# A two-layer relational graph convolution: separate PSUM banks for the halves of the turn, one bank for node sums, one DRAM table of sums for both layers

## The chip, the cores and the metric

The kernel runs on one core of one Trainium2 chip. The metric is the device time of one execution in microseconds (us). A line number such as L1712 is a line of the kernel file before the change. Engines: PE is TensorE, DVE is VectorE, ACT is ScalarE, POOL is GpSimd, SP is SyncE.

## The reference

There are 50000 nodes with 128 features, 50000 edges sorted by destination, each with 128 attributes and one of 8 types.

```python
h = relu(layernorm(x))
for l in range(2):
    m = relu(h[src] + edge_attr)                         # one row for each edge
    seg = edge_type * N + dst
    mean = segment_sum(m, seg) / max(count(seg), 1)      # a mean for each node and type
    h = einsum('rnd,rdo->no', mean.reshape(8, N, 128), weight[l]) + h @ root[l] + bias[l]
    h = batch_norm(h)                                    # over all nodes
    if l == 0: h = relu(h)
out = x + h
```

## The kernel before, in words

**Tiles and groups.** The edges are cut into 394 tiles of 127 (plus one of overlap); four tiles, far apart in the list, make one of NG = 99 groups. `tiles(g)` names the tiles of group g. Each layer l runs one loop over the groups, with all engines some groups apart; `gg = l * NG + g` counts on through both layers. A step of the loop is called step i here.

**What happens to a group.** POOL gathers the source rows of its four tiles with one indirect DMA each (L839) into a ring `hb`. In layer 0 DVE and ACT normalise them (L1145 to L1165, L1465); in layer 1 DVE scales and shifts them (L1179, L1180). DVE adds the edge rows, loaded by SP (L699), and signals `t_ready` (L1176, L1182). DVE also makes one matrix for each tile, `pm`, which orders the edges by type into 8 x 32 slots and scales them by one over the count (L1193, function `columns`, signal `set_ready`). Then comes **the turn** (function `turn`, L1702 to L1718): for each tile one product of 128x128 by 128x256 that turns the rows so that features lie on partitions and edges lie ordered by type. A group has two halves of two tiles, h = 0 and h = 1; each half fills one PSUM bank of 128x512. ACT takes a half out with Relu (function `message`, L1485, signal `m_ready`, two for each group). The end of half 0 is signalled as `half_ps`, of half 1 as `tr_ps`. **In the kernel before both halves go to the one bank `ps_turn` = `ps_t[0]`**, so each half waits for the message of the half before it (L1709: `m_ready` >= 2*gg + h).

After the turn PE multiplies by the weights of each type (`products`, L1745, banks `ps_y[0]` and `ps_y[1]`, signals `yh_ps` and `y_ps`), ACT copies each bank out (`products_out`, L1493), PE turns it back (`turned_back`, L1777, banks `ps_s`), ACT copies the first half (`first_half`, L1502) and DVE the second (`second_half`, L1257), and PE sums over edges of the same node with a 0/1 matrix `sm` that DVE made (`same_node`, L1219): `node_sums`, L1791, into `ps_o[gg % 2]`. ACT copies row 0 of these sums into the input of the next group (`carry`, L1515, signal `carried`) and the whole bank to a buffer `ob` (`sums_out`, L1524, signal `ob_ready`). POOL scatters `ob` to the table `acc[l]` with one indirect DMA for each tile (L854); for the tiles named WIDE, SP writes 112 rows with a plain DMA (L723). In layer 0, PE also makes one column of places for each tile and half (`place_column`, L1731, bank `ps_t[1]`, signal `place_ps`); in layer 1 it multiplies early rows by the root matrix (`first_rows` L1802, `first_product` L1807, bank `ps_t[1]`).

**Order by hand.** Each engine runs its instructions in the order in which they are written. PE's step i (L1810 to L1831) is: products(i, 0) with the place columns of group i+1 between them, turned_back(i-1, 0), turn(i+2, 0), [first_rows], products(i, 1), turned_back(i-1, 1), turn(i+2, 1), [first_product], node_sums(i-2). ACT's step i (L1539 to L1563) is: carry(i-2), sums_out(i-3), root_of(i+4), [first_turned, first_out], products_out(i, 0), first_half(i-1), message(i+2, 0), normalised(i+4), products_out(i, 1), message(i+2, 1), half_normalised(i+4). DVE's step i (L1278 to L1303) is: group_stats(i+4), edge_sum(i+3), columns(i+3), group_scales(i+4), same_node(i-1), places_in(i+1), second_half(i-1); the stats, scales and places are there in layer 0 only. In `columns`, DVE waits for `place_ps` of group i+1 (layer 0) before it overwrites `pm`.

**POOL's order** (L899 to L902): the scatters of group after group, with gathers put between them. Before the scatters of group g it waits for `ob_ready` (L845), and before the third tile's it waits for `tr_ps` >= gg + 6, the end of turn(g+5, 1) (L848).

**The tables of sums.** `acc` has two tables, one for each layer, of 25 MB each that must be zero where nothing is scattered. ACT zeroes `acc[0]` during the setup with 28 DMAs (L1449); SP zeroes `acc[1]` during the loop of layer 0, one DMA of 896 KB every third step (L744). After each loop, three rows are added where the streams of tiles meet (L882), and a pass over 49 chunks of nodes reads the table, adds the product with the root matrix and, in layer 0, stores the rows `h1_rows` for the next layer. All engines have a second program for edges that aren't sorted; with this input it isn't taken.

Of the kernel before, what the change touches and what calls it, by code (L numbers as in the profile page):

```python
# [41 lines left out]
def gnn_kernel(nc, x, src, dst, edge_attr, edge_type, weight, root, bias, gamma, beta, out):  # L42
# [105 lines left out]
    with ctx:  # L148
# [11 lines left out]
        acc = [dram(f"acc_{l}", [P * F + NTP * P, D]) for l in range(L)]  # L160
# [285 lines left out]
        ps_turn = ps_t[0]  # L446
# [219 lines left out]
        def _(sp):  # L666
# [36 lines left out]
            edge_rows(0, 0)  # L703
            edge_rows(1, 0)
# [109 lines left out]
        def _(pool):  # L814
# [74 lines left out]
            def layers(put):  # L889
# [17 lines left out]
            with pool.If(unsorted > 0):  # L907
# [10 lines left out]
                layers(scatter_alone)  # L918
# [14 lines left out]
        def _(dve):  # L933
# [186 lines left out]
            def in_order(sorted_):  # L1120
# [5 lines left out]
                def counts_in():  # L1126
                    dve.wait_ge(inv_ps, 5)
                    own.link(v.tensor_copy(inv_t[:, :], ps_t[1][:, :]))
                    own.link(v.memset(inv_t[0:1, :], 1.0))
# [73 lines left out]
                def places_in(g):  # L1203
                    w = len(tiles(g))
                    dve.wait_ge(place_ps, g + 1)
                    at = ps_t[1][:, 0:NH * H].rearrange("p (b j) -> p b j", b=NH)
# [64 lines left out]
                def join_rows():  # L1271
                    dve.wait_ge(join_to_ps, 1)
                    v.tensor_copy(join_at[:, :], ps_t[1][0:J, W4 - 1:W4]).then_inc(join_at_ready, 1)
# [159 lines left out]
        def _(act):  # L1433
# [43 lines left out]
            def message(g, h, l):  # L1477
# [7 lines left out]
                a_.activation(mt_at(gg)[:, a:b, :].rearrange("p j c -> p (j c)"), ps_turn[:, 0:(b - a) * RC],  # L1485
# [19 lines left out]
            def carry(g, l):  # L1505
# [7 lines left out]
                else:  # L1513
                    act.wait_ge(o_ps, sums_done(l, g - 1))
                    a_.activation(to, ps_o[(gg - 1) % 2][0:1, 0:w * D], ACT.Copy).then_inc(carried, 1)  # L1515

            def sums_out(g, l):
# [6 lines left out]
                a_.activation(ob[:, gg % OB, 0:w, :].rearrange("p w d -> p (w d)"), ps_o[gg % 2][:, 0:w * D],  # L1524
                              ACT.Copy).then_inc(ob_ready, 1)

            def first_turned(k):
# [3 lines left out]
                a_.activation(ht[:, k % 2, 0:W4], ps_t[1][:, :], ACT.Relu, scale=bn_col[:, 0, 0:1],  # L1531
                              bias=bn_col[:, 0, 1:2]).then_inc(ownT_ready, 1)

            def first_out(k):
                act.wait_ge(first_ps, k + 1)
                a_.activation(own_at(k // 2)[:, k % 2 * W4:(k % 2 + 1) * W4], ps_t[1][:, :], ACT.Copy).then_inc(first_ready, 1)
# [100 lines left out]
        def _(pe):  # L1637
# [57 lines left out]
            def program(sorted_):  # L1695
# [4 lines left out]
                cols(ps_t[1], tm_inv).then_inc(inv_ps, 1)  # L1700

                def turn(g, h, l):  # L1702
# [6 lines left out]
                    wait(pe, m_ready, 2 * gg + h)  # L1709
                    for j in range(a, b):  # L1710
                        if sorted_:
                            last = te.matmul(ps_turn[:, (j - a) * RC:(j - a + 1) * RC], hb[:, hb_slot(gg), j, :], pm[:, gg % 2, j, :],  # L1712
                                             start=True, stop=True)
                        else:
                            for c in range(NH):
                                k = (j - a) * RC + c * P
                                last = te.transpose(ps_turn[:, k:k + P], hb[:, hb_slot(gg), j, :], ident[:, :])
                    last.then_inc((half_ps, tr_ps)[h], 1)  # L1718

                def place_column(g, n):  # L1720
# [10 lines left out]
                    last = te.matmul(ps_t[1][:, k:k + 1], pm[:, g % 2, j, b * P:(b + 1) * P], ikey_t[:, t:t + 1], start=True, stop=True)  # L1731
# [50 lines left out]
                def node_sums(g, l):  # L1782
# [12 lines left out]
                def first_rows(k):  # L1795
# [4 lines left out]
                    for j in range(H):  # L1800
                        a = (k % 2 * H + j) * D
                        last = te.transpose(ps_t[1][:, j * D:(j + 1) * D], own_at(i)[:, a:a + D], ident[:, :])  # L1802
                    last.then_inc(ownT_ps, 1)

                def first_product(k):
                    pe.wait_ge(ownT_ready, k + 1)
                    te.matmul(ps_t[1][:, :], root_sb[:, D:2 * D], ht[:, k % 2, 0:W4], start=True, stop=True).then_inc(first_ps, 1)  # L1807
# [156 lines left out]
```

## Time and profile before

| what | us |
|---|---|
| median of 3 timed runs | 2876.24 |
| lowest and highest of them | 2862.11, 2884.39 |
| the profiled execution, its own time | 2859.57 |
| its span (first to last instruction) | 2857.8 |
| outside the span | 1.8 |

The profile is of one execution. Busy shares are of the span. In a row of the waits, "PE ps_t L1712 <- ACT arena L1485" means that PE stood idle before line 1712 until ACT's line 1485 released it. "remote" stands where the signal came at a time at which no recorded instruction ended, and "issue" where the engine waited for nothing that the profile shows.

### The profile page before, as it was taken

The numbers are of one execution on the slowest core, as the hardware profiler recorded it, in microseconds if no ns is written. First come the engines' busy times: TensorE is split into PE (matmuls) and PEld (weight loads), VectorE is DVE, ScalarE is ACT, GpSimd is POOL, SyncE is SP. The second block draws the span as 40 slices with busy tenths as digits, with TensorE's granted clock in tenths as the row PEclk, the third lists the DMA queues.
The fourth block names the chain that finished last, engine by engine and source line by source line (L and its number), as shares of the span: only waits on it lengthen the run. The fifth ranks groups of instructions, "written<-read, shape, count | busy, mean of one in ns | idle before, by whom it ended". The sixth has DMA issues, their size and how long they took to land. (4 is left out here: it accounts for less than half of the span.)

```text
span 2857.8 us, 43800 instructions
## 1 busy us (share of the span) xinstructions
PE 2128.6 (74%) x14404; PEld 1932.0 (68%) x14404; DVE 1557.2 (54%) x4526; ACT 1296.7 (45%) x2670; POOL 1406.9 (49%) x1377
## 2 busy tenths in 40 slices
PE   2168878777777777778996777887778787787966
PEld 0058777677677777767995666776667676677955
DVE  4565556555555555553786555554454454444754
ACT  0035556555555555554442344444343344343555
POOL 6405444555455555554003576676676677762100
PEclk9998999998988989988997898998898788998976
DMA  9423444444344433432996233322222233217889
GB/s 340 157 96 109 122 133 135 133 125 132 126 133 132 132 124 104 128 114 95 408 415 226 69 101 93 90 84 85 85 82 84 75 90 90 83 52 266 287 337 404
DMA packets 264672, 434.29 MB, mean 152 GB/s; under 512 B 39075, under 2 KB 170782, under 8 KB 264444
## 3 DMA queue, kind: packets, MB, share of 16 engines
q1 hardware_dynamic: 196598, 251.61, 26.0%
q0 software_dynamic: 46192, 99.84, 12.2%
q10 hardware_dynamic: 21654, 79.99, 6.9%
q8 instruction: 121, 1.98, 0.3%
q14 instruction: 107, 0.88, 0.1%
HBM read 255.41 MB, written 175.88 MB: 151 GB/s over the span
## 5 line engine op out<-in xcount | busy, mean ns | idle before, releaser
L854 POOL DMA_INDIRECT acc<-arena x550 | 585.6, 1065 | 732.8 <-PE ps_t L1712 454.8
L1712 PE MATMUL ps_t<-arena 128*128 128x256 f32 x1576 | 492.3, 441 | 414.0 <-ACT arena L1485 318.6
L1712 PEld LDWEIGHTS ps_t<-arena 128*128 128x128 f32 x1576 | 302.8, 214 | 490.4 <-ACT arena L1485 331.4
L839 POOL DMA_INDIRECT arena<-h_rows,arena x394 | 416.6, 1057 | 327.5 <-DMA h_rows<-chunk_mem 182.2
L1193 DVE TENSOR_SCALAR arena<-arena 128x256 f32<-128x256 f32 x788 | 274.6, 412 | 486.7 <-remote 414.6
L1745 PE MATMUL ps_y<-arena 128*128 128x128 f32 (+1 forms) x3168 | 518.1, 292 | 16.5 <-issue 16.1
L1791 PEld LDWEIGHTS ps_o<-arena 128*128 128x128 f32 x3152 | 476.1, 231 | 49.1 <-issue 33.4
L1493 ACT ACTIVATE arena<-ps_y 128x512 f32<-128x512 f32 (+1 forms) x396 | 231.4, 584 | 546.2 <-remote 489.1
L1791 PE MATMUL ps_o<-arena 128*128 128x128 f32 x3152 | 471.0, 313 | 7.5 <-issue 7.5
L1745 PEld LDWEIGHTS ps_y<-arena 128*128 128x128 f32 x3168 | 445.5, 201 | 27.9 <-issue 18.5
L839 POOL DMA_INDIRECT arena<-in_x_dram,arena x394 | 387.0, 982 | 135.8 <-issue 121.4
L1257 DVE COPY arena<-ps_s 128x512 f32<-128x512 f32 (+1 forms) x198 | 136.3, 689 | 361.9 <-remote 288.3
L1219 DVE TENSOR_TENSOR arena<-arena 128x512 f32<-128x512 f32 (+1 forms) x396 | 254.4, 684 | 110.9 <-remote 68.9
L1485 ACT ACTIVATE arena<-ps_t 128x512 f32<-128x512 f32 x396 | 233.4, 589 | 160.6 <-PE ps_t L1712 78.3
L1777 PE MATMUL ps_s<-ident,arena 128*128 128x128 f32 x1576 | 256.1, 281 | 28.8 <-issue 28.1
L1515 ACT ACTIVATE arena<-ps_o 1x512 f32<-1x512 f32 (+1 forms) x196 | 113.6, 580 | 303.1 <-remote 147.1
L1777 PEld LDWEIGHTS ps_s<-ident,arena 128*128 128x128 f32 x1576 | 195.5, 150 | 38.1 <-issue 37.9
L1731 PEld LDWEIGHTS ps_t<-arena 128*128 128x128 f32 x1576 | 214.7, 198 | 2.7 <-issue 2.5
L1731 PE MATMUL ps_t<-arena 128*128 128x1 f32 x1576 | 203.9, 233 | 2.9 <-issue 1.5
L1465 ACT ACTIVATE arena<-arena,nmr,rstd 128x128 f32<-128x128 f32 x394 | 162.1, 484 | 30.3 <-DVE nmr L1165 30.3
L1502 ACT ACTIVATE arena<-ps_s 128x512 f32<-128x512 f32 (+1 forms) x198 | 116.0, 586 | 92.1 <-PE ps_s L1777 46.0
L1524 ACT ACTIVATE arena<-ps_o 128x512 f32<-128x512 f32 (+1 forms) x198 | 112.4, 567 | 7.6 <-remote 5.6
(280 smaller groups left out, 2396.6 us busy)
## 6 DMA issues: line engine op xcount, KB each, us to landing
arena<-in_edge_attr_dram SPq DMA_DIRECT2D x190, 256.0 KB
chunk_mem<-acc SPq DMA_DIRECT2D x55, 512.0 KB, 13.2
acc<-arena ACTq DMA_DIRECT2D x28, 896.0 KB
acc<-arena SPq DMA_DIRECT2D x28, 896.0 KB
arena<-in_x_dram SPq DMA_DIRECT2D x45, 512.0 KB, 9.7
arena<-acc SPq DMA_DIRECT2D x43, 512.0 KB, 10.6
chunk_mem<-hn_rows SPq DMA_DIRECT2D x41, 512.0 KB
out_dram<-arena ACTq DMA_DIRECT2D x38, 512.0 KB, 9.2
```

What stands on the lines that cost most here:

```text
L839: pool.indirect_dma_start(out=hb[:, hb_slot(gg), t // NG, :], out_offset=None, in_=(x, h1_tab)[l], in_offset=at(src_t[:, t:t + 1])).then_i ...
L854: pool.indirect_dma_start(out=acc[l], out_offset=at(idx_t[:, t:t + 1]), in_=ob[:, gg % OB, t // NG, :], in_offset=None, **how).then_inc(co ...
L1193: ins = v.tensor_scalar(pm[:, gg % 2, j, :], iota_f[:, :], slot_t[:, t:t + 1], inv_t[:, t:t + 1], ALU.is_equal, ALU.mult)
L1219: ins = v.tensor_tensor(sm[:, gg % SM, b, 0:w, :], iota_f[:, 0:P].unsqueeze(1).to_broadcast([P, w, P]), place_at[:, g, b, 0:w].unsqueeze(2 ...
L1465: ins = a_.activation(row, row, ACT.Relu, scale=rstd[:, g % 2, j:j + 1], bias=nmr[:, g % 2, j:j + 1])
L1485: a_.activation(mt_at(gg)[:, a:b, :].rearrange("p j c -> p (j c)"), ps_turn[:, 0:(b - a) * RC], ACT.Relu).then_inc(m_ready, 1)
L1493: a_.activation(yts[:, gg % 2, b, 0:w, :].rearrange("p j e -> p (j e)"), ps_y[b][:, 0:w * D], ACT.Copy).then_inc(yt_ready, 1)
L1712: last = te.matmul(ps_turn[:, (j - a) * RC:(j - a + 1) * RC], hb[:, hb_slot(gg), j, :], pm[:, gg % 2, j, :], start=True, stop=True)
L1731: last = te.matmul(ps_t[1][:, k:k + 1], pm[:, g % 2, j, b * P:(b + 1) * P], ikey_t[:, t:t + 1], start=True, stop=True)
L1745: last = te.matmul(to[:, 0:w, q, :], w_sb[l][:, r * D:(r + 1) * D], mt_at(gg)[:, 0:w, r * CAP:(r + 1) * CAP], start=True, stop=True)
L1777: last = te.transpose(ps_s[b][:, c], yts[:, gg % 2, b, j, :], ident[:, :])
L1791: last = te.matmul(ps_o[gg % 2][:, c], sm[:, gg % SM, b, j, :], yb[:, gg % 2, b, j, :], start=b == 0, stop=b == NH - 1)
```

## The change

Six edits. (1) The turn's half h writes bank `ps_t[h]`, and its wait is one message shorter: half 0 waits for message(g-1, 0), half 1 for message(g-1, 1). (2) Node sums have one bank, `ps_o[0]`, so `node_sums` waits until sums_out of the group before it is done (`ob_ready` >= gg in place of gg - 1). (3) What used `ps_t[1]` (places, early rows, counts, joins) uses `ps_o[1]`, named `ps_side`. (4) Both layers scatter to one table `acc`; SP's 28 zeroing DMAs in layer 0 go, and so does POOL's wait for them. Both layers write the same rows of it, so that layer 1 overwrites what layer 0 left. (5) SP issues the edge rows of groups 2 and 3 with those of 0 and 1, ahead of its wait for the counts. (6) In the program for unsorted edges POOL zeroes the table again between the layers.

```diff
-        acc = [dram(f"acc_{l}", [P * F + NTP * P, D]) for l in range(L)]
+        acc = [dram("acc", [P * F + NTP * P, D])] * L
...
-        ps_turn = ps_t[0]
+        ps_sum = ps_o[0]
+        ps_side = ps_o[1]
...
-            edge_rows(0, 0)
-            edge_rows(1, 0)
+            for g in range(XB):
+                edge_rows(g, 0)
...
-                sp.wait_ge(acc_zero[l], 16 * ZN)
+                if l == 0:
+                    sp.wait_ge(acc_zero[0], 16 * ZN)
                 for n in range(NG):
-                    if l > 0 or n >= 2:
+                    if l > 0 or n >= XB:
                         edge_rows(n, l)
...
-                    if l == 0 and n % 3 == 0 and n // 3 < ZN:
-                        far = bass.AP(acc[1].tensor, (n // 3) * P * ZW, [[ZW, P], [1, ZW]])
-                        sp.dma_start(far, zeros[:, :]).then_inc(acc_zero[1], 16)
...
+            def zero_again():
+                for a in range(ZN):
+                    pool.dma_start(bass.AP(acc[1].tensor, a * P * ZW, [[ZW, P], [1, ZW]]), zeros[:, :]).then_inc(acc_zero[1], 16)
+                pool.wait_ge(acc_zero[1], 16 * ZN)
...
                         all_stored(pool)
+                        if again is not None:
+                            again()
...
-                        pool.wait_ge(acc_zero[1], 16 * ZN)
...
-                layers(scatter_alone)
+                layers(scatter_alone, zero_again)
...
                 # message (ACT)
-                a_.activation(mt_at(gg)[:, a:b, :]..., ps_turn[:, 0:(b - a) * RC],
+                a_.activation(mt_at(gg)[:, a:b, :]..., ps_t[h][:, 0:(b - a) * RC],
...
                 # carry and sums_out (ACT)
-                    a_.activation(to, ps_o[(gg - 1) % 2][0:1, 0:w * D], ACT.Copy).then_inc(carried, 1)
+                    a_.activation(to, ps_sum[0:1, 0:w * D], ACT.Copy).then_inc(carried, 1)
...
                 # turn (PE)
-                    wait(pe, m_ready, 2 * gg + h)
+                    wait(pe, m_ready, 2 * gg - 1 + h)
                     for j in range(a, b):
                         if sorted_:
-                            last = te.matmul(ps_turn[:, (j - a) * RC:(j - a + 1) * RC], hb[:, hb_slot(gg), j, :], pm[:, gg % 2, j, :],
+                            last = te.matmul(ps_t[h][:, (j - a) * RC:(j - a + 1) * RC], hb[:, hb_slot(gg), j, :], pm[:, gg % 2, j, :],
...
                 # node_sums (PE)
-                    wait(pe, ob_ready, gg - 1)
+                    wait(pe, ob_ready, gg)
...
-                            last = te.matmul(ps_o[gg % 2][:, c], sm[:, gg % SM, b, j, :], yb[:, gg % 2, b, j, :],
+                            last = te.matmul(ps_sum[:, c], sm[:, gg % SM, b, j, :], yb[:, gg % 2, b, j, :],
```

## Rows read from the trace of the kernel before

**Rows 1.** Page: busy time of each engine, share of the span, instructions.

```profile
PE 2128.6 (74%) x14404; PEld 1932.0 (68%) x14404; DVE 1557.2 (54%) x4526; ACT 1296.7 (45%) x2670; POOL 1406.9 (49%) x1377
```

**Rows 2.** Windows (us, each engine's busy us, granted clock, DMA share, GB/s).

```profile
230.00:1310.00 1080.00, 837.76 (x5775) 787.19 (x5773) 601.77 (x2537) 605.87 (x1407) 558.74 (x557) 0.90 0.41 125
...
1357.00:1510.00 153.00, 148.20 (x1321) 145.85 (x1321) 125.48 (x300) 67.42 (x146) 0.00 (x0) 1.00 1.02 412
...
1550.00:2580.00 1030.00, 783.62 (x4980) 689.19 (x4980) 509.70 (x975) 422.19 (x777) 696.95 (x648) 0.87 0.30 84
```

**Rows 3.** Windows of line 1524 alone, one sums_out for each step.

```profile
230.00:1310.00 1080.00, 51.23 (x90) 0.90 0.41 125
...
1550.00:2580.00 1030.00, 55.24 (x97) 0.87 0.30 84
```

**Rows 4.** Waits in 230 to 1310 us: total us, times, longest.

```profile
DVE arena L1193 <- remote: 387.9, 74, 7.9
POOL acc L854 <- PE ps_t L1712: 367.7, 90, 5.7
ACT arena L1493 <- remote: 309.8, 70, 6.8
...
PE ps_t L1712 <- ACT arena L1485: 220.1, 78, 5.0
```

**Rows 5.** Timeline, one step of layer 0, start, us, engine, line.

```profile
712.39 0.47 PE L1745 MATMUL ps_y<-arena 128*128 128x128 f32 x2
...
714.03 0.99 POOL L854 DMA_INDIRECT acc<-arena  x1 [0.30 <-issue]
...
716.33 0.60 ACT L1493 ACTIVATE arena<-ps_y 128x512 f32<-128x512 f32 x1 [4.45 <-remote]
716.82 0.59 ACT L1502 ACTIVATE arena<-ps_s 128x512 f32<-128x512 f32 x1
717.30 0.60 ACT L1485 ACTIVATE arena<-ps_t 128x512 f32<-128x512 f32 x1
717.96 1.13 PE L1712 MATMUL ps_t<-arena 128*128 128x256 f32 x4 [1.45 <-ACT arena L1485]
718.92 1.95 PE L1791 MATMUL ps_o<-arena 128*128 128x128 f32 x16
719.37 0.98 POOL L854 DMA_INDIRECT acc<-arena  x1 [4.35 <-PE ps_t L1712]
...
722.17 0.57 ACT L1515 ACTIVATE arena<-ps_o 1x512 f32<-1x512 f32 x1
722.64 0.57 ACT L1524 ACTIVATE arena<-ps_o 128x512 f32<-128x512 f32 x1
...
723.24 1.06 POOL L839 DMA_INDIRECT arena<-in_x_dram,arena  x1 [0.30 <-issue]
```

**Rows 6.** Waits in 1550 to 2580 us, the loop of layer 1.

```profile
PE ps_t L1712 <- ACT arena L1485: 91.2, 32, 11.7
...
POOL acc L854 <- PE ps_t L1712: 74.5, 32, 5.4
```

**Rows 7.** Timeline of PE inside a long run of POOL's DMAs, layer 1.

```profile
1934.27 0.37 PE L1777 MATMUL ps_s<-ident,arena 128*128 128x128 f32 x1 [0.63 <-issue]
1934.98 0.46 PE L1777 MATMUL ps_s<-ident,arena 128*128 128x128 f32 x1 [0.34 <-issue]
1935.69 0.37 PE L1777 MATMUL ps_s<-ident,arena 128*128 128x128 f32 x1 [0.25 <-issue]
```

**Rows 8.** Line 744 (zeroing), and the waits of SP's queue.

```profile
L744 SPq DMA_DIRECT2D acc<-arena x28: 18/432/1454, 160.9 to 1058.4; - x28
...
SPq L699 <- DVE arena L1176: 511.0, 61, 11.1
```

More of the change, by code:

```diff
@@ L887, in _, with layers @@
                 gather(g, t, 0)
-            def layers(put):
+            def zero_again():
+                for a in range(ZN):
+                    pool.dma_start(bass.AP(acc[1].tensor, a * P * ZW, [[ZW, P], [1, ZW]]), zeros[:, :]).then_inc(acc_zero[1], 16)
+                pool.wait_ge(acc_zero[1], 16 * ZN)
+            def layers(put, again=None):
                 for l in range(L):
@@ L1127, in counts_in @@
                     dve.wait_ge(inv_ps, 5)
-                    own.link(v.tensor_copy(inv_t[:, :], ps_t[1][:, :]))
+                    own.link(v.tensor_copy(inv_t[:, :], ps_side[:, :]))
                     own.link(v.memset(inv_t[0:1, :], 1.0))
@@ L1272, in join_rows @@
                     dve.wait_ge(join_to_ps, 1)
-                    v.tensor_copy(join_at[:, :], ps_t[1][0:J, W4 - 1:W4]).then_inc(join_at_ready, 1)
+                    v.tensor_copy(join_at[:, :], ps_side[0:J, W4 - 1:W4]).then_inc(join_at_ready, 1)
                 for l in range(L):
@@ L1530, in first_turned @@
                     act.wait_ge(first_ps, k - 1)
-                a_.activation(ht[:, k % 2, 0:W4], ps_t[1][:, :], ACT.Relu, scale=bn_col[:, 0, 0:1],
+                a_.activation(ht[:, k % 2, 0:W4], ps_side[:, :], ACT.Relu, scale=bn_col[:, 0, 0:1],
                               bias=bn_col[:, 0, 1:2]).then_inc(ownT_ready, 1)
@@ L1535, in first_out @@
                 act.wait_ge(first_ps, k + 1)
-                a_.activation(own_at(k // 2)[:, k % 2 * W4:(k % 2 + 1) * W4], ps_t[1][:, :], ACT.Copy).then_inc(first_ready, 1)
+                a_.activation(own_at(k // 2)[:, k % 2 * W4:(k % 2 + 1) * W4], ps_side[:, :], ACT.Copy).then_inc(first_ready, 1)
             for l in range(L):
@@ L1699, in program @@
                 pe.wait_ge(tminv_in, 32)
-                cols(ps_t[1], tm_inv).then_inc(inv_ps, 1)
+                cols(ps_side, tm_inv).then_inc(inv_ps, 1)
                 def turn(g, h, l):
@@ L1716, in turn @@
                                 k = (j - a) * RC + c * P
-                                last = te.transpose(ps_turn[:, k:k + P], hb[:, hb_slot(gg), j, :], ident[:, :])
+                                last = te.transpose(ps_t[h][:, k:k + P], hb[:, hb_slot(gg), j, :], ident[:, :])
                     last.then_inc((half_ps, tr_ps)[h], 1)
@@ L1730, in place_column @@
                     k = b * H + j
-                    last = te.matmul(ps_t[1][:, k:k + 1], pm[:, g % 2, j, b * P:(b + 1) * P], ikey_t[:, t:t + 1], start=True, stop=True)
+                    last = te.matmul(ps_side[:, k:k + 1], pm[:, g % 2, j, b * P:(b + 1) * P], ikey_t[:, t:t + 1], start=True, stop=True)
                     if n == NH * w - 1:
@@ L1801, in first_rows @@
                         a = (k % 2 * H + j) * D
-                        last = te.transpose(ps_t[1][:, j * D:(j + 1) * D], own_at(i)[:, a:a + D], ident[:, :])
+                        last = te.transpose(ps_side[:, j * D:(j + 1) * D], own_at(i)[:, a:a + D], ident[:, :])
                     last.then_inc(ownT_ps, 1)
@@ L1806, in first_product @@
                     pe.wait_ge(ownT_ready, k + 1)
-                    te.matmul(ps_t[1][:, :], root_sb[:, D:2 * D], ht[:, k % 2, 0:W4], start=True, stop=True).then_inc(first_ps, 1)
+                    te.matmul(ps_side[:, :], root_sb[:, D:2 * D], ht[:, k % 2, 0:W4], start=True, stop=True).then_inc(first_ps, 1)
                 for l in range(L):
@@ L1833, in program @@
                             pe.wait_ge(join_set, 1)
-                            te.matmul(ps_t[1][0:J, W4 - 1:W4], join_to[:, :], ones[0:1, 0:1], start=True, stop=True).then_inc(join_to_ps, 1)
+                            te.matmul(ps_side[0:J, W4 - 1:W4], join_to[:, :], ones[0:1, 0:1], start=True, stop=True).then_inc(join_to_ps, 1)
                         if sorted_ and l == 0 and i == -1:
```

6 lines of the change are left out of this document (3 added, 3 removed).

## The prediction, written before the changed kernel was run

> **What bounds the kernel now.** I read the page first: no engine is busy for more than 74% of the span [rows 1], so the time lies in waits. Then the windows by stage. The two loops over groups take 1080 us of layer 0 and 1030 us of layer 1; the pass between them is bound by DMA (share 1.02) and runs at the full clock [rows 2]. Line 1524 runs once for each step, so the windows hold 90 and 97 steps [rows 3]: a step is 1080 / 90 = 12.0 us in layer 0 and 1030 / 97 = 10.6 us in layer 1. Against that stand two floors. PE is busy for 837.76 / 90 = 9.3 us of a step and 783.62 / 97 = 8.1 us. POOL is busy for 558.74 us and has 0.30 us of issue ahead of each of its 557 instructions [rows 2, 5], together 726 us or 8.1 us a step; in layer 1 it is 696.95 + 648 x 0.30 = 891 us or 9.2 us a step. So layer 0 lies 2.7 us over its floor (PE) and layer 1 lies 1.4 us over its own (POOL).
>
> The waits of layer 0 say who waits for whom: POOL waits 367.7 us, 4.1 us a step, for the turn; PE's turn waits 220.1 us (78 times, 2.8 us each) for the message; ACT's products_out waits 309.8 us for something "remote" and DVE's columns 387.9 us [rows 4]. One step shows it as a ring [rows 5]. PE's last product that ACT waits for is listed to end at 712.86, but ACT starts its copy at 716.33. POOL's run of indirect DMAs ended at 715.02. The same order stands in the other steps that I read: PE's signals come late while POOL issues a run of DMAs, and go through about 1.3 us after it. From there: products_out, first_half, message (716.33 to 717.90), then turn 1 (717.96 to 719.09), then POOL's next run from 719.37. So the ring of a step is POOL's run, 1.3 us, 1.6 us of ACT, 1.1 us of turn, 0.3 us.
>
> The Trainium skill, Perfetto Trace Analysis, section "Tensor Engine Instruction (MATMUL, LD_WEIGHTS)", says that the end of a matmul in a profile is estimated, and that the signal goes out only after PSUM has acknowledged the writes. It gives a reason for a late signal; that one is late by 3.5 us only the row shows.
>
> **The change, part by part.**
>
> *Two banks for the turn.* Half 1 of group i+2 needed message(i+2, 0), which ACT runs behind products_out(i, 0), and so behind PE's late signal. Now it needs message(i+1, 1), done a step before. PE runs turn 1 straight behind turned_back(i-1, 1). The removed piece is the 1.45 us that PE stood idle in the step shown [rows 5], 2.8 us in the mean of the 78 waits [rows 4]; 220.1 us is the most that this wait itself can give in layer 0, and 91.2 us in layer 1 [rows 6]. What is late next? First PE's signal of turn 1, `tr_ps`: it can itself be held back by POOL's run, so POOL starts at the earliest when the held signals come, at 716.3 or, with turn 1 still to run, 717.5, in place of 719.37. Second, sums_out: the fourth DMA of POOL's run waits for `ob_ready`. It started at 723.24 and sums_out ended at 722.64 + 0.57 = 723.21 [rows 5], so it was on the brink; a POOL that starts 2 us sooner waits there 2 us. But in that pause PE's signals can get out, so that ACT and DVE find `yh_ps` and `place_ps` when they come to them, and aren't held until the whole run is over. So the step shortens, but by less than the wait removed, and the pauses of 4.1 us become shorter ones.
>
> For the size I take layer 1 as the pattern: there PE waits for the message in 32 of 97 steps only [rows 6], and a step takes 10.6 / 9.2 = 1.155 of its floor. The same factor on layer 0's floor gives 9.31 x 1.155 = 10.75 us, which is 1.25 us less than 12.0; by 90 steps 112 us. The bounds are nothing (the wait is handed on whole) and 12.0 - 9.31 = 2.7 us x 90 = 242 us (PE without a gap). In layer 1 the bounds are nothing and 1030 - 891 = 139 us (POOL without a gap); PE's wait of 91.2 us overlaps with POOL's of 74.5 us [rows 6], and I take about a third of it, 28 us, since POOL is already at 891 / 1030 = 87% there.
>
> *One bank for node sums.* node_sums(i-2) now waits for sums_out(i-3), which ACT runs right behind carry(i-2), for which PE waited anyway. The wait is longer by one copy of 0.57 us. In the step shown these copies lie at 710.7 to 711.8 and node_sums at 718.92, and the next pair at 722.2 to 723.2 [rows 5], so there are some 7 us of cover. PE stands behind that wait with products(i+1, 0), whose signals ACT and DVE need. With turn 1 out of the way node_sums comes perhaps 2 us sooner, which is still covered. I take 0; if all cover went, it would be 0.57 x 187 steps = 107 us, and a gain is excluded, as a wait is only added.
>
> *The side bank.* The same products and copies in another bank, which no one else uses in the loops: 0.
>
> *One table.* 28 DMAs of 896 KB go. At the 412 GB/s of the pass between the layers [rows 2] they are 25.7 MB / 412 GB/s = 62 us of all DMA engines, spread over a loop in which the DMA share is 0.41, and no instruction waited for them. SP issues them in 0.43 us each, 12 us in all, and has 511.0 us of waits for edge_sum before its edge rows [rows 8]. So 0, with 62 us as the most that could come back (if every transfer stood in the way of the gathers), and nothing below 0, for the only added accesses are writes of layer 1 to lines that were read a pass before. POOL's wait for the zeroing was long satisfied.
>
> *Edge rows of groups 2 and 3 earlier.* Two DMAs of 256 KB are moved ahead of SP's wait for the counts. They take 2 x 0.26 MB / 412 GB/s = 1.3 us from the zeroing in the setup, and may save as much at the first steps: 0, give or take 2 us. The unsorted program's zeroing isn't run.
>
> Sum: 2859.6 (the profiled execution) - 112 - 28 = 2719.6. The median of the timed runs lies 16.7 us over the profiled execution, so I predict 2736 us.
>
> **The rivals.**
>
> *A, the wait is handed on.* POOL, freed from the turn, waits at its fourth DMA for sums_out instead, and its run ends when it did before. For it: the 0.03 us between sums_out and that DMA [rows 5]. Against it: the pause lets the held signals out, and ACT's copies of 722.2 to 723.2 hang on the same ring. It gives 2876 us in layer 0 and up to 28 us less by layer 1: 2848 to 2876.
>
> *B, the full gain.* PE close to its floor in layer 0 (10.0 us a step, 180 us less) and two fifths of POOL's idle time in layer 1 (60 us less): 2636 us. For it: PE runs at 1.00 where it is busy for 148.2 of 153 us, and at 0.90 and 0.87 in the loops, where it is busy for 78% and 76% [rows 2]; with the gap gone from the loop the higher clock (2.4 GHz) may be granted for more of it and PE's 9.3 us shrink. Against it: late signals stay. The Trainium skill, TensorE: Matmul & The Clock Gate, section "Why this matters for your kernels", says that idle gaps between bursts of matmuls bring the lower clock. By that rule the gain is larger than the gap itself; the rows agree as far as they go.
>
> *C, slower.* POOL's pause for the turn is what lets PE's signals out. In a long run of POOL's DMAs in layer 1, PE issues one matmul in 0.71 us (1934.27, 1934.98, 1935.69) [rows 7]. If POOL's runs in layer 0 join to such long ones, turn 1 and node_sums, 20 matmuls that take 1.13 + 1.95 = 3.1 us [rows 5], take 20 x 0.71 = 14.2 us, 11 us more. It decides from 140 / 11 = 13 such steps in the 187; at 18 of them it is 198 - 140 = 58 us slower: 2934 us. For it: that is what layer 1 does at times. Against it: layer 1, with all that, is nearer to its floor than layer 0.
>
> *D, the edit doesn't bite.* PE waits at the same place for something else (turned_back needs the copies of the same ACT). That is A's time.
>
> **How the numbers follow.** The forecast has 0.53, with its own range from 2680 to 2800; B 0.17; A with D 0.22; C 0.08. The range that leaves out 2 in 10 goes from 2630 to 2868 us: it takes in B and most of A, leaves out C and the far ends of the bounds. About 1% (29 us) is what a measurement of this kernel can tell from no change. Faster by more than that: all of the forecast and B, and a small part of A, 0.73. Within 1%: 0.19. Slower: 0.08.
>
> **What the profile after would show.** Right: in layer 0 the wait of L1712 for L1485 is all but gone from its 220 us; POOL's wait for the turn falls from 367.7 us to under 200 and a wait of POOL for L1524 of 50 to 150 us appears; the step is 10.3 to 11.2 us; PE's clock in the loop is at or over 0.90; the pass between the layers and the end keep their lengths within 5 us; the DMA share of layer 0 falls to about 0.36 with no effect. Wrong: the wait moves to L1777 or L1745 with the step still at 12 us (A, D); matmuls at 0.7 us with "issue" ahead of them in layer 0 (C); the gain lies in the setup or the passes, which would mean that the table or the zeroing was worth something after all; or layer 1 gains more than layer 0, which would mean that the pattern was read from the wrong layer.

## The result, and the profile after

| | before | after |
|---|---|---|
| median, us | 2869.18 (4 runs, 2859.66 to 2884.39) | 2684.66 (4 runs, 2683.28 to 2688.29) |
| ratio | | 0.9354, 95% interval 0.9306 to 0.9402 |
| profiled execution, span | 2857.8 | 2681.5 |

The changed kernel is 184.5 us faster and takes 2684.66 us. The forecast was a gain of 140 us and a time of 2736 us. In the spans (176.3 us) it lies as follows; the marks are ACT's first and last copy of node sums (L1524, now L1528) in each layer.

| stretch | before | after | difference |
|---|---|---|---|
| start to the first copy of layer 0 | 209.9 | 204.3 | -5.6 |
| loop of layer 0, first to last copy | 1133.4 | 995.6 | -137.8 |
| between the loops | 255.4 | 247.4 | -8.0 |
| loop of layer 1 | 989.9 | 963.1 | -26.8 |
| last copy to the end | 269.2 | 271.1 | +1.9 |

The page of the changed kernel, answering to [rows 1]:

```profile
PE 2115.1 (79%) x14404; PEld 1913.1 (71%) x14404; DVE 1554.1 (58%) x4526; ACT 1287.3 (48%) x2670; POOL 1424.4 (53%) x1377
```

The same work in less time: busy times are within 1.3% of before. Its windows, answering to [rows 2] (length, then busy us of PE, PEld, DVE, ACT, POOL, clock, DMA share, GB/s):

```profile
225.00:1164.00 939.00, 828.97 (x5735) 769.14 (x5734) 599.62 (x2531) 597.05 (x1404) 561.21 (x554) 0.91 0.41 120
...
1218.00:1368.00 150.00, 147.68 (x1319) 145.51 (x1318) 123.37 (x292) 67.32 (x145) 0.00 (x0) 1.00 1.03 417
1408.00:2402.00 994.00, 774.14 (x4942) 682.34 (x4941) 504.90 (x969) 417.36 (x771) 703.55 (x643) 0.86 0.30 86
```

and of its line 1528 alone, answering to [rows 3]:

```profile
225.00:1164.00 939.00, 50.67 (x89) 0.91 0.41 120
1408.00:2402.00 994.00, 54.66 (x96) 0.86 0.30 86
```

A step of layer 0 takes 939 / 89 = 10.55 us (12.0 before), one of layer 1 994 / 96 = 10.35 us (10.6). PE's work in a step of layer 0 is 828.97 / 89 = 9.31 us, just as before, and the granted clock went from 0.90 to 0.91: the clock gave nothing back.

The waits of the changed kernel in the loop of layer 0, answering to [rows 4]:

```profile
DVE arena L1197 <- remote: 269.4, 47, 8.2
ACT arena L1497 <- remote: 209.2, 43, 7.2
POOL acc L852 <- PE ps_t L1716: 139.0, 62, 5.4
...
POOL arena L837 <- ACT arena L1528: 65.6, 38, 3.0
...
PE ps_s L1781 <- issue: 21.8, 39, 1.1
PE ps_o L1735 <- issue: 19.9, 22, 1.7
PE ps_o L1795 <- issue: 19.8, 34, 1.0
PE ps_t L1716 <- issue: 18.8, 37, 1.1
...
PE ps_y L1749 <- issue: 15.5, 24, 1.2
```

The turn's wait for the message (220.1 us in [rows 4]) is gone from the list. POOL's wait for the turn fell from 367.7 to 139.0 us, and its wait for sums_out rose from 8.6 to 65.6 us. ACT and DVE still wait for late signals, but 219 us less together.

Something new stands in front of PE: waits on "issue" in the middle of its own work, 95.8 us in the five rows above, against 21.8 us in all such rows of the kernel before. PE's idle time in the two windows fell from 1080 - 837.76 = 242.2 us to 939 - 828.97 = 110.0 us. So of the 220.1 us of the removed wait some 133 us are saved; 74 us came back as "issue" and 12.9 us as a wait ahead of the place columns (L1735) for DVE.

The timeline of the changed kernel shows two kinds of step, answering to [rows 5]:

```profile
704.21 0.99 POOL L852 DMA_INDIRECT acc<-arena  x1 [1.40 <-ACT arena L1528]
...
708.25 0.60 PE L1781 MATMUL ps_s<-ident,arena 128*128 128x128 f32 x4
708.69 1.03 PE L1716 MATMUL ps_t<-arena 128*128 128x256 f32 x4
...
709.55 1.95 PE L1795 MATMUL ps_o<-arena 128*128 128x128 f32 x16
...
710.00 0.99 POOL L852 DMA_INDIRECT acc<-arena  x1 [3.52 <-PE ps_t L1716]
...
713.27 0.47 PE L1749 MATMUL ps_y<-arena 128*128 128x128 f32 x2
...
716.16 0.60 PE L1781 MATMUL ps_s<-ident,arena 128*128 128x128 f32 x4
...
716.60 1.28 PE L1716 MATMUL ps_t<-arena 128*128 128x256 f32 x4
...
718.65 0.60 ACT L1497 ACTIVATE arena<-ps_y 128x512 f32<-128x512 f32 x1 [5.71 <-remote]
```

In both, turn 1 (L1716) follows turned_back (L1781) without a gap. In the second the signal for ACT's products_out (L1497) is late again: PE's last product of that half is listed to end at 713.27 + 0.47 = 713.74 and ACT starts at 718.65, 4.9 us later. But PE had begun turn 1 at 716.60, two us before ACT was let go. Before, PE sat still there until ACT's third copy was done.

### The profile page after: what moved, and what is told of

The parts are those of the page before. It is cut to its first block and busy times, and to the rows that moved or that the text cites. A ratio compares the mean times of both kernels' runs of the same rounds, so it can differ in the third digit from the quotient of the medians.

```text
span 2681.5 us, 43771 instructions
## 1 busy us (share of the span) xinstructions
PE 2115.1 (79%) x14404; PEld 1913.1 (71%) x14404; DVE 1554.1 (58%) x4526; ACT 1287.3 (48%) x2670; POOL 1424.4 (53%) x1377
## 3 DMA queue, kind: packets, MB, share of 16 engines
q0 software_dynamic: 46192, 99.84, 12.9%
## 5 line engine op out<-in xcount | busy, mean ns | idle before, releaser
L1749 PE MATMUL ps_y<-arena 128*128 128x128 f32 (+1 forms) x3168 | 556.1, 305 | 59.0 <-issue 47.8
L1749 PEld LDWEIGHTS ps_y<-arena 128*128 128x128 f32 x3168 | 476.9, 212 | 84.1 <-issue 72.6
L1716 PE MATMUL ps_t<-arena 128*128 128x256 f32 x1576 | 476.2, 423 | 49.7 <-issue 41.8
L837 POOL DMA_INDIRECT arena<-in_x_dram,arena x394 | 393.9, 1000 | 184.1 <-issue 112.1
L1795 PEld LDWEIGHTS ps_o<-arena 128*128 128x128 f32 x3152 | 409.2, 200 | 113.9 <-issue 103.4
L1795 PE MATMUL ps_o<-arena 128*128 128x128 f32 x3152 | 424.6, 285 | 65.9 <-issue 61.6
L1197 DVE TENSOR_SCALAR arena<-arena 128x256 f32<-128x256 f32 x788 | 274.5, 412 | 310.4 <-remote 285.7
L1497 ACT ACTIVATE arena<-ps_y 128x512 f32<-128x512 f32 (+1 forms) x396 | 230.7, 583 | 409.6 <-remote 352.7
L1716 PEld LDWEIGHTS ps_t<-arena 128*128 128x128 f32 x1576 | 304.7, 214 | 100.5 <-issue 73.4
L1781 PE MATMUL ps_s<-ident,arena 128*128 128x128 f32 x1576 | 274.9, 296 | 39.9 <-issue 39.1
L1735 PEld LDWEIGHTS ps_o<-arena 128*128 128x128 f32 x1576 | 221.1, 203 | 42.9 <-issue 41.8
L1781 PEld LDWEIGHTS ps_s<-ident,arena 128*128 128x128 f32 x1576 | 212.4, 160 | 49.3 <-issue 49.1
L1735 PE MATMUL ps_o<-arena 128*128 128x1 f32 x1576 | 212.9, 239 | 35.8 <-issue 21.0
L1528 ACT ACTIVATE arena<-ps_o 128x512 f32<-128x512 f32 (+1 forms) x198 | 112.4, 567 | 5.8 <-issue 3.1
```

What stands on the lines that cost most here:

```text
L837: pool.indirect_dma_start(out=hb[:, hb_slot(gg), t // NG, :], out_offset=None, in_=(x, h1_tab)[l], in_offset=at(src_t[:, t:t + 1])).then_i ...
L1197: ins = v.tensor_scalar(pm[:, gg % 2, j, :], iota_f[:, :], slot_t[:, t:t + 1], inv_t[:, t:t + 1], ALU.is_equal, ALU.mult)
L1497: a_.activation(yts[:, gg % 2, b, 0:w, :].rearrange("p j e -> p (j e)"), ps_y[b][:, 0:w * D], ACT.Copy).then_inc(yt_ready, 1)
L1716: last = te.matmul(ps_t[h][:, (j - a) * RC:(j - a + 1) * RC], hb[:, hb_slot(gg), j, :], pm[:, gg % 2, j, :], start=True, stop=True)
L1735: last = te.matmul(ps_side[:, k:k + 1], pm[:, g % 2, j, b * P:(b + 1) * P], ikey_t[:, t:t + 1], start=True, stop=True)
L1749: last = te.matmul(to[:, 0:w, q, :], w_sb[l][:, r * D:(r + 1) * D], mt_at(gg)[:, 0:w, r * CAP:(r + 1) * CAP], start=True, stop=True)
```

## The experiments

Each run had the kernel before beside it on the same chip. They were made in five lots (e1 to e4 on chip 8, e5 and e6 on chip 1, e7 to e10 on chip 2, e11 on chip 9, e12 on chip 9), and the chip turned out to matter more than any edit: on chips 8 and 2 the kernel before took 2350 us, on chips 1 and 9 it took 2858 to 2867, near to the 2869 of the result above (the record doesn't name the chip of those runs). So the table comes first. Each chip but chip 9 was used for one lot only, so whether this is a trait of a chip or a state that a chip can be in at a time isn't shown; "kind of chip" below means no more than that the kernel before takes 2350 us on it or some 2860.

| run | edit | ratio to before, 95% interval | before on that chip |
|---|---|---|---|
| e1 | banks alone | 0.9974 (0.9962 to 0.9987) | 2350.1 |
| e2 | table alone | 1.0006 (0.9994 to 1.0018) | 2350.1 |
| e3 | changed, old wait | 0.9993 (0.9982 to 1.0005) | 2350.1 |
| e4 | changed, no pause of POOL | 0.9959 (0.9942 to 0.9976) | 2350.1 |
| e5 | changed, again | 0.9374 (0.9340 to 0.9408) | 2858.5 |
| e6 | before, again | one run, 2850.8 us | 2858.5 |
| e7 | as e3 | 0.9995 (0.9981 to 1.0010) | 2350.3 |
| e8 | as e4 | 0.9955 (0.9941 to 0.9970) | 2350.3 |
| e9 | changed, no scatters | one run, 2044.0 us | 2350.3 |
| e10 | changed, lead of 9 groups | 1.0451 (1.0420 to 1.0482) | 2350.3 |
| e11 | as e3 | 1.0004 (0.9982 to 1.0025) | 2866.8 |
| e12 | as e10 | 0.9380 (0.9347 to 0.9413) | 2859.4 |

**e1, the bank edits alone.** The changed kernel with edits 4 to 6 taken back:

```diff
-        acc = [dram("acc", [P * F + NTP * P, D])] * L
+        acc = [dram(f"acc_{l}", [P * F + NTP * P, D]) for l in range(L)]
...
+                    if l == 0 and n % 3 == 0 and n // 3 < ZN:
+                        far = bass.AP(acc[1].tensor, (n // 3) * P * ZW, [[ZW, P], [1, ZW]])
+                        sp.dma_start(far, zeros[:, :]).then_inc(acc_zero[1], 16)
...
-            for g in range(XB):
-                edge_rows(g, 0)
+            edge_rows(0, 0)
+            edge_rows(1, 0)
```

> The kernel before with the bank edits alone (halves of the turn in two banks, one bank for node sums, the side bank); two tables, zeroing and edge rows as before. Theory (the gain comes from the turn's wait): ratio to before 0.935 to 0.945, step of layer 0 about 10.6 us against 12.1. Rival (the table and the 25 MB less of writes carry part of the gain): ratio 0.95 or more, with a step of layer 0 of 11 us or more.

Measured: 2345.24 us against 2350.09. **e2, one table alone**, the kernel before with

```diff
-        acc = [dram(f"acc_{l}", [P * F + NTP * P, D]) for l in range(L)]
+        acc = [dram("acc", [P * F + NTP * P, D])] * L
...
-                    if l == 0 and n % 3 == 0 and n // 3 < ZN:
-                        far = bass.AP(acc[1].tensor, (n // 3) * P * ZW, [[ZW, P], [1, ZW]])
-                        sp.dma_start(far, zeros[:, :]).then_inc(acc_zero[1], 16)
```

> The kernel before with one table for both layers and no zeroing in layer 0, and nothing else. Theory: within 0.5% of before, since the steps with a zeroing DMA were no longer than the others (11.9 to 12.3 us against 12.1). Rival: 1% to 2% faster, up to the 62 us that 25.7 MB take at 412 GB/s.

Measured: 2352.05 us, no difference: 25.7 MB less of writes are worth nothing there. **e3, the old wait** in the changed kernel:

```diff
-                    wait(pe, m_ready, 2 * gg - 1 + h)
+                    wait(pe, m_ready, 2 * gg + h)
```

> The changed kernel with the old wait put back ahead of each half of the turn (two banks, but each half still waits for the message just before it). Theory (the wait is the whole cause): the time of before, ratio 0.99 to 1.00, with L1716 waiting some 220 us for the message in layer 0. Rival (the other edits or their placement matter): ratio below 0.98.

Measured: 2348.94 us. **e4, no pause of POOL:**

```diff
-                if t // NG == 2 and g + 5 < NG:
-                    pool.wait_ge(tr_ps, gg + 6)
```

> The changed kernel without POOL's wait for the end of a later group's turn ahead of the third tile's scatter. That wait guards no data. Theory (PE's signals are held back while POOL issues a run of indirect DMAs, and go through in the pauses): POOL's runs get longer, PE's signals come later, and layer 0 gains nothing or gets slower, 0 to 60 us. Rival (POOL is simply short of time, and each pause of it is lost): layer 0 gains most of the pause, 80 to 130 us, ratio to before 0.90 or less.

Measured: 2341.20 us. None of the four can be held against its theory as it was meant, since before itself took 2350 us here in place of 2869. e1 missed its ratio of 0.935 to 0.945; its 0.9974 lies where the rival had it, but with a step of 8.4 us (760 / 90) and not of 11. e2 came out as expected. e3 has the ratio expected, but 34.5 us of waiting for the message in layer 0 in place of 220. e4 is 9 us under before, far from its rival's ratio of 0.90; its theory compares it with the changed kernel, which wasn't run on this chip. The wait is in the code of e3, and costs next to nothing. Why is seen in its waits in the loop of layer 0, 155 to 915 us:

```profile
POOL arena L837 <- issue: 94.7, 311, 0.3
DVE st L1149 <- DMA arena<-in_x_dram,arena: 68.1, 25, 5.2
...
DVE arena L1197 <- PE ps_o L1735: 57.8, 66, 1.8
...
ACT arena L1497 <- PE ps_y L1749: 36.6, 64, 1.1
...
PE ps_t L1716 <- ACT arena L1489: 34.5, 21, 3.8
```

There is no "remote" in front of ACT's L1497 or DVE's L1197: the signals come when PE's instructions end. The message is there when the turn wants it, in all but 21 cases. The windows of e3:

```profile
155.00:915.00 760.00, 725.53 (x5764) 701.60 (x5764) 607.59 (x2543) 604.47 (x1406) 562.45 (x559) 0.99 0.52 149
1180.00:2060.00 880.00, 721.63 (x4867) 654.44 (x4867) 490.58 (x946) 411.30 (x757) 688.28 (x630) 0.93 0.33 95
```

PE is busy for 95% of layer 0's loop, and 89 steps take 760 us, 8.5 us each. With prompt signals layer 0 is bound by PE for the most part. The kernel before itself left no profile on such a chip; e2, which is the kernel before but for the table, has PE busy for 720.20 of the same 760 us. Its timeline, with the same instructions as [rows 5]:

```profile
503.73 0.47 PE L1749 MATMUL ps_y<-arena 128*128 128x128 f32 x2
504.04 0.50 PE L1735 MATMUL ps_o<-arena 128*128 128x1 f32 x4
504.24 0.60 ACT L1497 ACTIVATE arena<-ps_y 128x512 f32<-128x512 f32 x1 [0.54 <-PE ps_y L1749]
...
504.97 0.99 POOL L837 DMA_INDIRECT arena<-in_x_dram,arena  x1 [0.30 <-issue]
...
505.94 0.60 ACT L1489 ACTIVATE arena<-ps_t 128x512 f32<-128x512 f32 x1 [0.27 <-PE ps_t L1716]
```

The last product of half 0 ends at 504.20 and ACT starts at 504.24, while POOL is in the midst of its DMAs; in [rows 5] the same step took from 712.86 to 716.33. An indirect DMA takes POOL 0.987 us in the median in e3 and 0.984 before: it isn't POOL's speed that differs.

The trace also records when each semaphore changes. I matched each PE instruction that sends a signal with the next change of its semaphore (pairs over 8 us apart left out as missing records), and asked whether the instruction's listed end lay within a run of POOL's indirect DMAs (gaps under 0.6 us). This is my own count, not a view of the profile:

```
                       within POOL's runs         outside
                     signals  late > 0.3 us    signals  late > 0.3 us
before                 1170      77%             719      11%
after                  1106      68%             720      12%
e6  before  (chip 1)   1177      79%             693       9%
e11 old wait (chip 9)  1146      76%             728      14%
e1  banks   (chip 8)   1509     0.3%             502       0%
e3  old wait (chip 8)  1509     0.3%             501       0%
```

**e5 and e6, the two kernels of the change again.**

> The changed kernel again, for the four runs before this took 2341 to 2352 us on a chip on which the kernel before takes 2350 us, not 2869, and on which PE's signals were on time in their traces. Theory (the change pays only where PE's signals are held back while POOL issues its DMAs): where they are on time, ratio 0.995 to 1.00; where they are late again, 0.93 to 0.94. Rival (the gain belongs to the change on any chip, and something in the four kernels lost it): 0.94 to 0.96 with signals on time.

> The kernel before once more, for a profile on the same chip as the run above. Theory: if PE's signals are on time, the step of layer 0 is 8.5 us, ACT's wait in front of L1493 for a remote signal is near 0 us against 489 us, and PE waits less than 60 us for the message at L1712 although the wait is in the code. If they are late, 12.1 us and the old waits. Rival (the chip is faster in some other way): shorter instructions of POOL or PE, or a higher clock, with the same waits.

Chip 1 had late signals, and the ratio 0.9374 is that of the result. So the gain repeats there, and the count above shows the lateness with it. PE's waits on "issue" in the loop of layer 0 repeat too: 105.3 us in e5. e6's step of layer 0 is 1080 / 90 = 12.0 us (12.1 was expected for late signals) and its turn waits 249.6 us for the message; e6's indirect DMAs take 0.987 us in the median, the same as on chip 8, so the rival (shorter instructions on the faster chips) is out for POOL's DMAs. PE's instructions are another matter: the clock granted in layer 0 is 0.91 in e6 and 0.99 in e3, so part of the faster chips' time is the clock's.

**e7, the old wait, and e8, no pause, once more,** with the edits of e3 and e4.

> The changed kernel with the old wait ahead of each half of the turn, as in e3, in the hope of a chip with late signals. Theory: where PE's signals are late (before at about 2860 us), ratio 0.985 to 1.00, layer 0's step at 12.0 us, for the wait of the turn is what lets a late signal cost time twice; where they are on time, 0.999 as in e3. Rival (the table, the edge rows or the banks' places carry part of the 6.3%): ratio 0.95 to 0.98 where signals are late.

> The changed kernel without POOL's wait for the turn, as in e4. Theory (late signals go through in POOL's pauses): where they are late, layer 0's step is 10.6 to 11.5 us, so 0 to 80 us slower than the changed kernel, and ratio to before 0.937 to 0.965. Rival (each pause of POOL is lost time): step under 10 us, ratio 0.91 or less. Where signals are on time, 0.996 as in e4.

They went to chip 2, with signals on time, and repeat e3 and e4: 0.9995 and 0.9955. What POOL's pause is worth where signals are late wasn't measured.

**e9, no scatters.**

```diff
+                if not add:
+                    pool.sem_inc(scat_out[gg % OB], 16)
+                    return
```

> The changed kernel without the 550 indirect scatters of the loops (it leaves those sums out of the table; gathers and everything else stay). POOL then has 4 DMAs a step, 5.2 us, in place of 8 to 9 us. Theory: where signals are late, they are late only within the shorter runs of gathers; the share of late PE signals falls from 46% to under 30%, and both steps come down to PE's own work, 8.5 to 9.5 us in layer 0 (from 10.6) and 8 to 9 in layer 1 (from 10.0). Rival (lateness has nothing to do with POOL): the share stays at 45% or more and the steps within 0.5 us of 10.6 and 10.0. Where signals are on time: layer 0 stays at 8.3 to 8.5 us (PE), and layer 1 falls from 9.3 to about 8.

Also on chip 2. Its windows, within the loops:

```profile
155.00:890.00 735.00, 733.24 (x5920) 713.97 (x5919) 609.84 (x2562) 617.03 (x1427) 299.26 (x309) 1.00 0.46 132
1150.00:1770.00 620.00, 620.00 (x4651) 578.22 (x4651) 468.95 (x906) 380.78 (x727) 413.78 (x353) 1.00 0.37 103
```

PE has no idle time left: 7.9 us a step in layer 0 (93 copies) and 6.7 us in layer 1 (92). So with prompt signals layer 0 (8.5 us in e3) is PE's for the most part: it fell by 0.6 us, to just under the 8.3 to 8.5 us expected. Layer 1 (9.2 us, 880 / 96) is POOL's, which with its issue is taken for 688.28 + 630 x 0.30 = 877 of those 880 us; there the fall went further than the 8 us expected. The clock is at 1.00, the higher level of 2.4 GHz, where PE never stops.

**e10, a shorter lead of the gathers.**

```diff
-    LEAD, LAST_LEAD = (20, 9), 8
+    LEAD, LAST_LEAD = (9, 9), 8
```

> The changed kernel with the gathers of 9 groups ahead of the loop of layer 0 in place of 20: 44 indirect DMAs, 57 us of POOL's time, move from the setup into the loop. Theory: where signals are late, the setup's signals between PE and DVE are freed 57 us earlier, so the first sums_out comes at 150 to 170 us in place of 204, and the loop pays some of it back (0.6 us a step of POOL): total 10 to 40 us faster than the changed kernel. Where signals are on time nothing is freed, and the loop of layer 0, near POOL's and PE's floor, gets 0 to 50 us longer. Rival (the setup's length is DVE's own work or the zeroing): first sums_out at 195 us or later and the total no better.

Chip 2 again: 2451.75 us, 4.5% or 101 us slower than before, where 50 us at most were expected. The first copy comes at 137.5 us (146.5 in e3) and the loop pays it with interest, 920.7 us against 805.0; DVE's wait for the gathered rows, 68.1 us in e3, has grown:

```profile
DVE st L1149 <- DMA arena<-in_x_dram,arena: 219.0, 79, 7.0
```

**e11, the old wait where signals are late.**

> The changed kernel with the old wait ahead of each half of the turn, a third time: e3 and e7 ran where signals are on time, and there the wait costs nothing (0.999 and 1.000). What is open is what it costs where signals are late. Theory: before at about 2860 us there, this ratio 0.985 to 1.00, layer 0's step at 12.0 us, L1716 waiting over 200 us for L1489 in layer 0. Rival (the other edits carry the gain): ratio 0.95 to 0.98. Where signals are on time: 0.999 once more.

Chip 9: 2864.68 us against 2866.77. This is the experiment that was wanted from the first: with all the other edits in place, and the one wait as it was, nothing of the 6.3 to 6.5% is left. The changed kernel itself wasn't run on chip 9, but with a shorter lead (e12) it has a ratio of 0.9380 there. Its waits in 230 to 1310 us are those of [rows 4] again:

```profile
POOL acc L852 <- PE ps_t L1716: 371.8, 90, 5.8
ACT arena L1497 <- remote: 335.2, 70, 6.9
...
PE ps_t L1716 <- ACT arena L1489: 224.8, 79, 5.0
```

It shows that without the shorter wait the gain isn't there: the banks, the single bank of node sums, the one table, the missing zeroing and the earlier edge rows together are worth nothing (interval 0.9982 to 1.0025) as long as the old wait stands. It doesn't show that they stay worthless once the wait is gone; the bank edits alone (e1) were never run where signals are late, so that they suffice for the whole gain is argued and not shown. The small gain in the setup goes with the wait: the first copy comes at 209.9 us in before, 208.9 in e6 and 209.0 in e11, and at 204.3 us in after and 204.1 in e5. The 8.0 us between the loops don't: that stretch takes 255.4 us in before and 249.7 in e6, 247.4 in after and 250.0 in e5, and 253.3 in e11, so from run to run it differs by nearly as much.

**e12, does POOL's issuing hold the signals back?** The edit of e10, on chip 9.

> The changed kernel with a lead of 9 groups of gathers ahead of layer 0's loop in place of 20, as in e10, in the hope of a chip with late signals. There the signals of the setup come late as long as POOL issues its 80 gathers (the first sums_out at 204 us, against 143 to 148 us on the other chips). Theory (POOL's issuing holds the signals back): POOL's run in the setup is 44 DMAs or 57 us shorter, DVE's and PE's chain is freed as much earlier, and the first sums_out comes at 150 to 175 us; the loop of layer 0 pays 100 to 140 us, as in e10 (1.4 us a step), or less, since it is longer anyway. Rival (that chip's signals are late by themselves, whatever POOL does): first sums_out at 195 us or later. Where signals are on time: first sums_out at 137 us and ratio 1.045, as in e10.

In the setup DVE and PE hand eight matrices to and fro (DVE L1031) while POOL gathers ahead. In e3, with signals on time, six of them take 3.68 us:

```profile
26.30 1.28 DVE L1031 SCALAR_TENSOR_TENSOR arena<-arena,ps_s 128x512 bf16<-128x512 f32 x2
28.74 3.68 DVE L1031 SCALAR_TENSOR_TENSOR arena<-arena,ps_s 128x512 bf16<-128x512 f32 x6 [1.15 <-PE ps_s L1663]
```

In e11, with late ones, each comes 5.6 us after the one before. Further on DVE's own signals come late too: its steps at L1087, 0.49 us apart in e3, follow one another at 1.4 us, as long as POOL issues (its last gather ends at 109.90 + 0.94 = 110.84 us) and some us beyond:

```profile
49.50 0.69 DVE L1031 SCALAR_TENSOR_TENSOR arena<-arena,ps_s 128x512 bf16<-128x512 f32 x1 [4.94 <-issue]
55.10 0.69 DVE L1031 SCALAR_TENSOR_TENSOR arena<-arena,ps_s 128x512 bf16<-128x512 f32 x1 [4.91 <-remote]
60.70 0.69 DVE L1031 SCALAR_TENSOR_TENSOR arena<-arena,ps_s 128x512 bf16<-128x512 f32 x1 [4.92 <-issue]
...
109.90 0.94 POOL L837 DMA_INDIRECT arena<-in_x_dram,arena  x1 [0.30 <-issue]
...
111.77 0.57 DVE L1087 SCALAR_TENSOR_TENSOR arena<-chunk_mem 128x392 f32<-128x392 f32 x1 [1.31 <-issue]
113.18 0.08 DVE L1087 DVE_READ_ACCUMULATOR arena<-chunk_mem 128x1 f32 x1 [0.84 <-issue]
...
119.47 0.57 DVE L1087 SCALAR_TENSOR_TENSOR arena<-chunk_mem 128x392 f32<-128x392 f32 x1
119.96 0.08 DVE L1087 DVE_READ_ACCUMULATOR arena<-chunk_mem 128x1 f32 x1
```

In e12, on the same chip, POOL's last gather ahead of the loop is issued at 54.21, and the lateness goes with it:

```profile
54.21 0.94 POOL L837 DMA_INDIRECT arena<-in_x_dram,arena  x1 [0.30 <-issue]
```

```profile
52.21 0.69 DVE L1031 SCALAR_TENSOR_TENSOR arena<-arena,ps_s 128x512 bf16<-128x512 f32 x1 [4.91 <-remote]
57.81 0.69 DVE L1031 SCALAR_TENSOR_TENSOR arena<-arena,ps_s 128x512 bf16<-128x512 f32 x1 [4.91 <-remote]
...
60.71 0.69 DVE L1035 COPY arena<-ps_t 128x512 f32<-128x512 f32 x1 [2.15 <-PE ps_t L1676]
...
63.25 0.15 DVE L1044 TENSOR_TENSOR near_end<-arena 1x1 f32<-1x1 f32 x1 [0.74 <-PE ps_s L1679]
```

The releasers are named again from 60.71 on. The first copy comes at 161.0 us, 43 us before that of the changed kernel (204.3) and 48 us before that of e11 on the same chip (209.0), for 55.7 us less of POOL's run (109.9 - 54.21); in e10, with signals on time, the same edit moves it by 9 us (137.5 against 146.5 in e3). The rival is out. Nor is it the zeroing of the table that holds the signals: from 60 to 80 us of e12 it keeps the DMA share at 1.02, and DVE is busy for 17.64 of these 20 us, against 6.11 in the changed kernel, where POOL is still gathering. Whether it is POOL's issuing or the gathers' own transfers that do it can't be told from these runs, for the edit moves both. The loop of layer 0 then takes 1041.5 us against 995.6 and eats the gain: the total is 2681.31 us, the same as the changed kernel's 2679.59 and 2684.66 on its chips.

## Why the prediction was right, and what it didn't see

*The removed wait.* Right, and shown: e11 puts it back and the whole gain is gone. It was 220.1 us in layer 0; 133 us of PE's idle time there went, and 87 us came back as "issue" and as a wait for DVE. On POOL's side the prediction named the wait for sums_out, put it at 50 to 150 us (65.6), and had POOL's wait for the turn fall under 200 us (139.0).

*The sizes.* Layer 0's term was 10.75 us a step and 112 us; measured are 10.55 us and 138 us. By the prediction's own count it is 1.45 us in each of 90 steps, 130 us; the other 8 us lie in the steps at the loop's ends, which that count leaves out. The factor of 1.155 over PE's floor, taken from layer 1, came out at 10.55 / 9.31 = 1.133. Nothing ties the two layers' factors together, for that of layer 1 stands over POOL's floor; that it came so near is luck as far as the runs show. So is layer 1's term, 28 us, a third of a wait by choice, which measured 26.8 (29.4 from e6 to e5). The total of 140 us fell 44.5 us short: 26 in layer 0 and 12 in the setup, between the loops and at the end, less 1 in layer 1; the other 8 are there because the profiled executions differ by 176.3 and the medians by 184.5 us. The time of 2684.66 us is no nearer to the 2736 forecast (51 us) than to B's 2636 (49 us). It is the step of 10.55 us, where B had 10.0 and the forecast 10.75, the 26.8 us in layer 1, where B had 60, and the clock that speak for the forecast.

*The edits put at nothing.* Right as far as e2 (signals on time) and e11 (late, with the old wait) go. That the node sums' bank has cover shows in the changed kernel itself: in its whole profile PE waits for sums_out before node_sums (L1795) for 2.3 us in two cases. The DMA share, which the prediction had at 0.36 in layer 0, stayed at 0.41, because the same bytes less 22 MB (135 to 113 MB) went over a shorter loop; in e11, where the loop kept its length, it is 0.36. The stretch between the loops shrank by 8.0 us, not under 5, which the spread between runs allows.

*The clock.* Rival B would have had PE's own work shrink. PE was busy for 9.31 us of a step before and after, and the clock granted in layer 0, a mean of stretches at 1.2 and at 2.4 GHz, went from 0.90 to 0.91, though PE's busy share rose from 78% to 88%. The Trainium skill, TensorE: Matmul & The Clock Gate, section "Why this matters for your kernels", says that idle gaps between bursts of matmuls bring the lower clock. In e3's layer 0, where PE is busy for 95%, the clock is 0.99 and the same work takes 725.53 / 89 = 8.15 us, which agrees with that; but e3's layer 1 has 0.93 at 82%, more than the changed kernel's layer 0 at 88%, so the busy share alone doesn't tell the clock. What would have raised it here isn't shown.

*Signals held back by POOL.* The prediction read this from a few steps and "remote" in the waits, and took it for a trait of the kernel. That POOL's gathers are what holds them in the setup, e12 shows; for the loops there is the count above. The 1.3 us after POOL's run fit 39% of the late signals of before (1.0 to 1.6 us after the end of the run in which they fell due, by the same count); 47% come while the run still lasts. But on chips 8 and 2 there is none of it. A forecast of 2736 us with a gain of 140 would have been far off there: before takes 2350 us, e1 with the bank edits gains 0.3%, and no other part of the change is worth anything. The changed kernel itself wasn't run on such a chip; e1 and e2 together, 0.9974 x 1.0006, put it at 0.998 there if the parts add up.

*Rivals.* A was partly true (the 65.6 us) without deciding. C, matmuls slowed by longer runs of POOL, came in part: PE's waits on "issue" rose from 21.8 to 95.8 us in the loop of layer 0, and matmuls that start 0.68 to 0.74 us after the one before, 8 in before, are 44 in after. In e3, with signals on time, PE has no such wait on "issue" there. The forecast had no term for it. It took a third of the removed wait and not all of it, so the sign of the change stayed.

## What to carry to other kernels

A "remote" releaser in front of an instruction whose sender had ended microseconds earlier is a late signal; look at what GpSimd issues at that time, and compare a second chip before the kernel is tuned around it. Where signals may be late, look first for a wait between two engines that runs both ways within a step: here a second PSUM bank that makes the wait one step older, with the other edits, removed 6.3 to 6.5%, though the same wait costs about 0.3% where signals are prompt (e1). Of what a removed wait took, count on a part only: of 220 us some 133 were saved here. DMAs that nothing waited for, 25.7 MB in this kernel, went without an effect on the time in the two cases in which that was tried (e2, e11).

## What the runs showed of the hardware that was not expected

- Two times for one and the same kernel: 2350 us (chips 8 and 2) and 2858 to 2869 us (chips 1 and 9, and the first runs), 22% apart, with POOL's DMAs equally long (0.987 and 0.984 us).
- On the second kind 77% of PE's signals that are due within POOL's runs of indirect DMAs are over 0.3 us late, 11% of those outside; on the first kind 0.3% and none. In the setup of the second kind DVE's signals come late too (e11: listed end 110.46, signal 111.77), so that its steps follow at 1.4 us. Why these chips do it, no run here shows.
- On the second kind PE stands idle between its own instructions with nothing in the profile that it waits for: 95.8 us in the changed kernel's loop of layer 0, 20.2 us in e11's with the old wait, none in e3's on the first kind.
- PE's granted clock in layer 0 is 0.99 on the first kind (e3, PE busy for 95%) and 0.90 on the second (before, 78%); with PE never idle (e9) it is 1.00.
- The zeroing, 28 DMAs of 896 KB, had no effect with prompt signals (e2), and none with late ones beside the other edits and the old wait (e11).
